# Reordering the front of a two-layer cross-attention kernel: load queues, K by halves, output operand on GpSimd, roots by pair, and the first score slots

## The reference

```python
q, k, v = tgt @ Wq.T, memory @ Wk.T, memory @ Wv.T        # per head, 16 heads
x = x + attention(q, k, v)[0]                             # sequence 0 alone, added to all 32
norm_X   = layernorm(ctx) * norm1_w + norm1_b
norm_F_L = layernorm(x)   * norm2_w + norm2_b
attended = softmax(norm_F_L @ norm_X.T * scale) @ norm_X
cross    = gelu(attended @ fc1_w.T + fc1_b) @ fc2_w.T + fc2_b
norm_c   = layernorm(cross) * norm3_w + norm3_b
out      = norm_F_L + gamma2 * (cross + gamma1 * softmax(norm_c @ norm_c.T * scale) @ norm_c)
```

## Time and profile before

| | |
|---|---|
| median of 3 runs | 245.54 us (245.11 to 245.64) |
| the profiled execution | 245.04 us, its span 243.1 us |
| PE busy in the span | 219.4 us (90%) |
| DVE busy | 187.5 us (77%) |
| ACT busy | 151.6 us (62%) |
| POOL busy | 140.6 us (58%) |
| DMA moved | 26.81 MB |

### The profile page before, as it was taken

How to read it: one execution, slowest core, us unless ns; L and a number is a source line. 1 busy time by engine, 2 the same in 40 slices (tenths; PEclk the granted TensorE clock), 3 DMA queues, 4 the chain that set the end, 5 groups by cost and what they waited for, 6 DMA issues and landing times.

```text
span 243.1 us, 5101 instructions
## 1 busy us (share of the span) xinstructions
PE 219.4 (90%) x1812; PEld 161.4 (66%) x1812; DVE 187.5 (77%) x363; ACT 151.6 (62%) x292; POOL 140.6 (58%) x212
## 2 busy tenths in 40 slices
PE   6989989697999999999999899999989988979860
PEld 6856647475878789787896777967667654454420
DVE  6888858899999987798799999933423767857773
ACT  2166866216778768776787976855684646657520
POOL 6000086676999999969878957500079885201340
PEclk9999999989999999999999999999999999999985
DMA  5990000154553525544145000000000024333468
GB/s 164 377 368 3 1 1 3 44 173 131 173 174 100 161 90 173 175 133 164 52 172 173 3 0 4 0 1 3 0 3 1 0 96 156 141 131 140 171 230 326
DMA packets 14712, 26.81 MB, mean 110 GB/s; under 512 B 1760, under 2 KB 1760, under 8 KB 14688
## 3 DMA queue, kind: packets, MB, share of 16 engines
q1 hardware_dynamic: 14688, 26.50, 32.0%
HBM read 18.11 MB, written 8.39 MB: 109 GB/s over the span
## 4 chain that ended last, share of the span: by engine, by line
PE 61%; DVE 20%; POOL 6%; issue 6%; ACT 5%; DVEq 0%; ACTq 0%; POOLq 0%
PE psum L1042 16%; PE psum L979 8%; PE psum L934 6%; PE psum L1050 5%; DVE bn L372 5%; DVE xN L392 5%; PE psum L1080 3%; PE psum L1160 2%; PE psum L1062 2%; PE psum L992 2%; DVE Fall L586 2%; DVE nmax L531 2%; PE psum L1007 2%; PE psum L1020 2%; PE psum L949 2%
## 5 line engine op out<-in xcount | busy, mean ns | idle before, releaser
L1042 PE MATMUL psum<-XT,Fall 128*128 128x256 f32 x256 | 62.5, 388 | 1.8 <-ACT Fall L822 1.8
L1042 PEld LDWEIGHTS psum<-XT,Fall 128*128 128x128 f32 x256 | 47.2, 195 | 7.6 <-ACT Fall L822 2.2
L665 POOL TENSOR_SCALAR cN<-cN,nmean,rstd 128x256 f32<-128x256 f32 x64 | 38.9, 618 | 2.4 <-POOL rstd L652 2.3
L645 POOL TENSOR_TENSOR xN<-xN,tgt 128x512 f32<-128x512 f32 x28 | 35.7, 1277 | 1.6 <-DVE xN L392 1.6
L845 ACT ACTIVATE PT<-psum 128x512 f32<-128x512 f32 x32 | 19.2, 599 | 24.4 <-PE psum L1050 24.2
L392 DVE TENSOR_SCALAR xN<-xN,bn,rstd 128x256 f32<-128x256 f32 x64 | 33.7, 571 | 0.7 <-POOL rstd L652 0.7
L652 POOL TENSOR_TENSOR rstd<-vps,minus_half 128x8 f32<-128x8 f32 (+1 forms) x16 | 25.0, 1564 | 15.2 <-DVE vps L383 15.1
L852 ACT ACTIVATE E<-psum,nmax 128x256 f32<-128x256 f32 x64 | 26.8, 476 | 10.7 <-DVE nmax L531 10.6
L531 DVE TENSOR_REDUCE nmax<-psum 128x2 f32<-128x512 f32 x32 | 22.0, 686 | 13.9 <-PE psum L1042 13.3
L934 PE MATMUL psum<-ident 128*128 128x128 f32 x198 | 29.9, 297 | 2.8 <-POOL ident L617 1.9
L934 PEld LDWEIGHTS psum<-ident 128*128 128x128 f32 x198 | 25.4, 201 | 7.2 <-issue 5.2
(11 more groups left out here) (174 smaller groups left out, 357.0 us busy)
## 6 DMA issues: line engine op xcount, KB each, us to landing
cN<-ctx SPq DMA_DIRECT2D x32, 256.0 KB, 3.0
xN<-x SPq DMA_DIRECT2D x32, 256.0 KB, 4.0
out<-Fall SPq DMA_DIRECT2D x32, 256.0 KB, 2.3
x0T<-x0t SPq DMA_DIRECT2D x1, 256.0 KB, 2.7
wqT<-wqt SPq DMA_DIRECT2D x1, 256.0 KB, 3.1
c0T<-c0t SPq DMA_DIRECT2D x1, 256.0 KB, 4.0
wkT<-wkt SPq DMA_DIRECT2D x1, 256.0 KB, 4.9
wvT<-wvt SPq DMA_DIRECT2D x1, 256.0 KB, 5.0
```

The costliest lines, as they stand in the source:

```text
L645: pool.tensor_tensor(xN[:, b % SLOTS, :], xN[:, b % SLOTS, :], tgt2[:, :, :].rearrange("p t d -> p (t d)"), ALU.add).then_inc(y_ok, 1)
L665: pool.tensor_scalar(own, own, nmean[:, p % 4, NT * m + t:NT * m + t + 1], root_of(p, 0, m, t), ALU.add, ALU.mult)\
L1042: last = pe.matmul(bank[SBANK1[b % 3]][:, t * N:(t + 1) * N], Fall[:, b, c, t * P:(t + 1) * P], XT[:, p % 4, c, m * N:(m + 1) * N], start= ...
```

## The change

It has these parts:

- **Loads.** ACT issues `x0T` and `c0T`; SP issues the parameters, the three weights, then all eight context sequences, then all eight x sequences.
- **Start of PE.** The dummy products use `meanw`, which is now GpSimd's first memset, and are eight instead of seven.
- **K by halves.** K's two halves go to two banks with a semaphore step each; DVE masks the first half before the first scores and the second half in slot 0. V's first half is projected behind the first scores and its second half in slot 2; ACT copies them in slots 1 and 3.
- **Operand products.** They move from the front of PE to the place behind the turned context pairs, with `project(0)`, seven dummy products and `project_back(0)` around them (there were 11 dummy products there). DVE copies their result ahead of its first `normal`.
- **Output operand.** It leaves DVE (7 small instructions ahead of the K mask, 4 behind it, 4 in slot 18) and becomes 17 small instructions on GpSimd behind its memsets.
- **Roots by pair.** The first six context sequences get variances, root and normalisation pair by pair within the attention slots.
- **Score slots.** DVE takes `maximum(b)` first in every slot. Statistics and x-side normals of the first slots come later and are caught up in slots 4 and 5. POOL's `add(5)` waits for the fourth DVE normal.

The diff, cut to its core:

```diff
@@ sync
-        for dst, src, arrived in ((x0T, x0t, q_in), (wqT, wqt, q_in), (c0T, c0t, k_in), (wkT, wkt, k_in),
-                                  (wvT, wvt, v_in)):
-            sp.dma_start(dst[:, :, :], src).then_inc(arrived, 16)
+        sp.dma_start(wqT[:, :, :], wqt).then_inc(q_in, 16)
+        sp.dma_start(wkT[:, :, :], wkt).then_inc(k_in, 16)
+        sp.dma_start(wvT[:, :, :], wvt).then_inc(v_in, 16)
+
+        for src, dst, arrived in ((c_d, cN, c_in), (x_d, xN, x_in)):
+            for b in range(SLOTS):
+                sp.dma_start(dst[:, b, :], src[b, :, :]).then_inc(arrived[b], 16)
@@ vector
-        output_operand(0)
-        dve.wait_ge(k_mm, 1)
-        for e, m in enumerate(("even", "odd")):
-            dve.tensor_scalar(kTm[:, e, :, :], tiles(bank[1]), c_(m), None, ALU.mult).then_inc(kT_ok, 1)
+        def masked(o):
+            dve.wait_ge(k_mm, o + 1)
+            for e, m in enumerate(("even", "odd")):
+                dve.tensor_scalar(kTm[:, e, o, :], bank[(1, 5)[o]][:, 0:N], c_(m), None, ALU.mult).then_inc(kT_ok, 1)
...
         add(2)
         add(3)
+        dve.wait_ge(qk_mm, 1)
+        link(dve.tensor_copy(Q[:, :], bank[7][:, 0:(H + 1) ** 2]))
+        link(dve.tensor_copy(K[:, :], bank[7][:, 64:64 + U * U]), "QK")
         normal(0)
         normal(1)
...
-        statistics(5, 1)
-        variances(2)
...
         for b in range(B):
             k, m, q = b // 2, b % 2, b // 4
-            if k + 3 < PAIRS:
-                statistics(b + 6, 0)
-                statistics(b + 6, 1)
-                if m == 1:
-                    variances(k + 3)
             maximum(b)
...
-            if k + 2 < PAIRS:
+            if b == 0:
+                statistics(2 * EARLY - 1, 1)
+                variances(EARLY - 1)
+            if b in (2, 3, 4):
+                normal(b + 3)
+            if 1 <= b <= 4:
+                statistics(b + 5, 0)
+                statistics(b + 5, 1)
+                if m == 0:
+                    variances((b + 5) // 2)
+            if b >= 4 and b + 6 < B:
+                statistics(b + 6, 0)
+                statistics(b + 6, 1)
+                if m == 1:
+                    variances((b + 6) // 2)
+            if b == 1:
+                normal(4)
+            elif b == 5:
+                normal(8)
+                normal(9)
+            elif 6 <= b < B - 4:
                 normal(b + 4)
@@ gpsimd
+        pool.memset(meanw[:, :], 1.0 / D).then_inc(consts, 1)
...
+            if b == 5:
+                pool.wait_ge(zy_ok, 8)
...
-        for b in range(2 * EARLY):
-            normal(b)
+        for p in range(EARLY):
+            pool.wait_ge(vps_first, 2 * p + 2)
+            pool.tensor_tensor(rstd[:, p, 0, :], vps[:, p, 0, :], minus_half[:, 0:2 * NT], ALU.pow).then_inc(root_first, 1)
+            normal(2 * p)
+            normal(2 * p + 1)
@@ scalar
+        act.dma_start(x0T[:, :, :], x0t).then_inc(q_in, 16)
+        act.dma_start(c0T[:, :, :], c0t).then_inc(k_in, 16)
@@ tensor
-        keep_busy(11, 7)
...
+        project(0)
+        operand_products()
+        keep_busy(3, 0)
+        project_back(0)
+        keep_busy(4, 0)
         turned(0, 1)
```

More of the change, by code:

```diff
@@ L52 @@
 QUADS = B // 4
+EARLY = 3
 SLOT = 64
@@ L338, in _ @@
                                        src[:, c, :].unsqueeze(1).to_broadcast([P, n, n]), ALU.mult), "prods")
[L340 to L352, removed]
-        output_operand(0)
-        dve.wait_ge(k_mm, 1)
-        for e, m in enumerate(("even", "odd")):
-            dve.tensor_scalar(kTm[:, e, :, :], tiles(bank[1]), c_(m), None, ALU.mult).then_inc(kT_ok, 1)
[L358 to L361, removed]
+        def masked(o):
+            dve.wait_ge(k_mm, o + 1)
+            for e, m in enumerate(("even", "odd")):
+                dve.tensor_scalar(kTm[:, e, o, :], bank[(1, 5)[o]][:, 0:N], c_(m), None, ALU.mult).then_inc(kT_ok, 1)
+        masked(0)
         stats = [0]
@@ L408, in _ @@
             if p < NHP:
+                if p == 0:
+                    masked(1)
                 if p < 2 * EARLY:
                     statistics(p, 0)
[L411 to L418, removed]
+                if p in (1, 3, 5):
+                    first_variances(p // 2)
         dve.wait_ge(o0_mm, NHP // 2)
@@ L638, in _, with step @@
         pool.memset(sC[:, :, SC:SLOT], 0.0).then_inc(zero_ok, 1)
+        oc = [0]
+        def step(ins):
+            ins.then_inc(operand_ok, 1)
+            oc[0] += 1
+            pool.wait_ge(operand_ok, oc[0])
+        a5 = c_("a5").rearrange("p (c k) -> p c k", c=DC)
+        pool.wait_ge(zero_ok, 4)
+        pool.wait_ge(alg, ALG["prods"])
+        step(pool.tensor_tensor(g12[:, :], c_("g1"), c_("g2"), ALU.mult))
+        for c in range(DC):
+            step(pool.tensor_scalar(Rt[:, c, 0:H], a5[:, c, 0:H], c_("g2", c), None, ALU.mult))
+            step(pool.tensor_scalar(Rt[:, c, H:CO], MT[:, c, :], g12[:, c:c + 1], None, ALU.mult))
+            step(pool.tensor_scalar(Rcut[:, c, 0:1], a5[:, c, H:H + 1], c_("g2", c), None, ALU.mult))
+            step(pool.tensor_tensor(Rt[:, c, CO - 1:CO], Rt[:, c, CO - 1:CO], Rcut[:, c, 0:1], ALU.add))
+        for part in range(2):
+            to = stR[:, :, part, :]
+            step(pool.tensor_copy(slots(to, CO, SLOTS_L[0]), repeated(Rt[:, :, :], 3)))
+            step(pool.tensor_tensor(Rcut[:, :, :], Rt[:, :, :], to[:, :, 0:CO], ALU.subtract))
+            step(pool.tensor_copy(slots(to, CO, SLOTS_L[1]), repeated(Rcut[:, :, :], 2)))
+            step(pool.tensor_tensor(to[:, :, 5 * CO:6 * CO], Rcut[:, :, :], to[:, :, 3 * CO:4 * CO], ALU.subtract))
+        ALG["stR"] = oc[0]
         def add(b):
@@ L862, in _ @@
             evacuate(p, 0)
+        turned_values(0)
         evacuate(0, 1)
@@ L870, in _ @@
             exponentials(b)
-            if b % 4 == 1:
+            if b % 4 == 1 and q >= 1:
                 turned_values(q)
```

86 lines of the change are left out of this document (48 added, 38 removed).

## The result

The changed kernel takes 251.39 us in the median of 4 runs (250.08 to 251.98), against 245.59 (245.11 to 247.34) for the kernel before in the same series. The ratio is 1.0225, with a 95% interval of 1.0182 to 1.0269: slower, by 5.8 us. The forecast was 250.6 us, and its range of 243.5 to 252.8 holds the time. The profiled execution took 251.32 us with a span of 249.4; before, the span was 243.1.

What follows compares the result with a forecast made beforehand. DVE was taken to bound the x-side preparation, PE the score slots. On 245.04 us: -0.6 (X3 earlier), +3.8 (chain to X4), +3.5 (clock), -1.05 (late slots) = +5.6, so 250.6 us; range 243.5 to 252.8.

Steps and rivals of the forecast that it cites:

- Front, 1.9 us of t0: From the span's start to DVE's first x-side normal: that normal was forecast about 1.9 us earlier than 44.12.
- t0: Start of DVE's first x-side normal, at 44.12 us in the kernel before; forecast about 1.9 us earlier.
- t0 to X3, 20.2 us: First x-side normal to the turn of context pair 3: forecast 20.2 us, 1.3 more than before.
- X3: Start of PE's turn of context pair 3, at 63.00 us before; forecast about 0.6 us earlier.
- X3 to X4, 11.3 us by the chain: Turn of context pair 3 to that of pair 4: everything in a row, 11.3 us against 7.49, 3.8 lost.
- X4: Start of PE's turn of context pair 4, at 70.49 us before; forecast 11.3 us behind X3.
- Two clock falls, 3.5 us: Scores behind X3 and X4: PE's longer waits lower its clock, costing 2 x 1.76 = 3.5 us; bounds 0 and 5.5.
- Late slots, -1.05 us: Slots 20 to 29: maximum ahead of statistics frees PE of waits of 0.80 and 0.25 us, 1.05 gained.
- one fall: Rival on the chain from X3 to X4: only one clock fall on the path, 249.0 us; one or none, chance 0.25.
- The first score also falls: Rival: first score at the lower clock, first two maxima and X3 1 us later, 251.6 us; included in 0.52.
- late loads: Rival in the front: loads land late, 1 us less gain, 251.6 us; included in the 0.52.
- The chain is covered: Rival: PE sets X4 again if X3 is before about 59.3, front's gain stays, 242.1 us; chance 0.18.

Runs made afterwards that it cites:

- waits filled: Changed kernel with seven dummy products on PE in each of the two waits ahead of and within the turn of context pair 3: 250.88 us, ratio 1.0227.
- old front with the new slots: Kernel before, with only the new order of statistics, variances and normals in DVE's score slots: 254.25 us, ratio 1.0374.
- five edits: The three edits, with four and two dummy products, plus sequence 6's statistics in slot 0 and GpSimd's normal 7 ahead of add(9), on the changed kernel: 244.33 us.
- old order from slot 6: Changed kernel with statistics and variances ahead of the maximum again from slot 6 on: 249.15 us, ratio 1.0149.
- one queue: Changed kernel with x0T and c0T issued by SP again, so all loads in one queue: 254.12 us in one run.
- nine edits: The five edits plus sequence 8's statistics earlier, normal 7 in slot 3, GpSimd's normal 9 ahead of add(11), dummy products around side x, pair 2: 242.95 us.
- three edits: Changed kernel with sequence 9's statistics and pair 4's variances in slot 3, dummy products in pair 3's waits, old order from slot 6: 245.36 us.

## Why the prediction came out right

The direction, the place and nearly the size: +5.8 us measured, +5.6 summed. By its steps:

- *Front, 1.9 us of t0:* measured 1.63. The first scores came 0.3 later than counted, since Q's products took 2.57 us, where I had counted on some of the time at a higher clock. The granted clock reads 1.00 all through the front, so no row shows such a change there. The adds (1.29) and the copies' short wait (0.24) were as counted.
- *t0 to X3, 20.2 us:* measured 20.10. The four points that were named on the way came as told: normals 2 and 3 in 1.38, the first maximum at 47.94 (48), DVE's wait for `add(5)`, the root of pair 3 at 57.19 (t0 + 14.70).
- *X3 to X4, 11.3 us by the chain:* 13.17 with the clock, and 10.98 if the turn and the score behind X3 are put at their full-clock times (1.33 to 0.87, 3.66 to 1.93). The waits of DVE and POOL show the ring, and moving two statistics and two small instructions cuts it. The kernel with the waits filled measured 10.82 for the same chain.
- *Two clock falls, 3.5 us:* **mis-sized.** One fall, on the path, of 2.2 us (1.73 in the score and 0.46 in the turn; 2.35 by the kernel with the waits filled). I had taken the waits ahead of X3 and X4 to be alike and each to bring a fall. In the profile after only the first did; in that of the old front with the new slots only the second did.
- *Late slots, -1.05 us:* **wrong in sign**, +1.0 measured. The step failed where it took PE's waits for ACT's copies as the end of a chain through DVE's maximum. The longer one lies in a stretch in which ACT works without a wait, two table loads among it, and it stayed. What the new order did was to put the variances behind the maximum, which made POOL's roots and normals later, and PE waited for these too.

With one fall of 2.2 and late slots of +1.0 the sum would have been -0.4 + 3.5 + 2.2 + 1.0 = 6.3, the difference of the spans. The two errors (1.3 too much, 2.1 too little) happened to cancel for the most part: that the number came so close is luck in these two terms, while the chain from X3 to X4 came as it was worked out.

The rival that came nearest was "one fall", at 249.0; with the late term as measured it would have read about 251. "The first score also falls" did not come (2.00 us at 45.90), nor did late loads. "The chain is covered" failed at its own condition: X3 was 62.59, not before 59.3 (59.2, by its own terms). The sentence of the Trainium skill that stood with it ("Perfetto Trace Analysis", section "Identifying Performance Opportunities") is not borne out here by the busy share alone: DVE was the busiest (9.93 of 10 us) and was relieved of 1.9 us. Of that 0.9 showed between t0 and X3, by the kernel without the wait of `add(5)`, and the time went up all the same, since a new chain of waits took more.

Open: why the same waits bring a fall of the clock in one execution and not in another. The waits of 1.10 and 0.84 ahead of the score of slot 3 were followed by one in two profiles (five edits: 55.43, and the old order from slot 6) and not in five others. Of the six profiles with the waits of 0.41 and 1.80 ahead of X4, three had a fall at X3 and none at X4 (after, old order from slot 6, no wait of add(5)), three the reverse (old front, waits filled, one queue). Late in the span the clock fell at 224 us with one queue and at 231 with the waits filled, behind waits of PE of 0.30 to 0.55 us that the changed kernel has too, without a fall.

## What to carry to other kernels

When an instruction is moved behind a wait on an in-order engine, write down what the awaited engine itself waits for: here DVE's variances moved behind a maximum, the maximum needs PE, PE needs GpSimd, and GpSimd needs the variances, so four links that had run side by side came one after the other. Put what only feeds a later stage (statistics, roots) into the idle time ahead of such a wait, and the short thing that the next engine stands waiting for first; one order for all slots was not the best in either kernel. And an edit that brings one stage forward is worth only what the next bound leaves of it: the same front brought X3 forward by 2.9 us with one order of the slots and by 0.7 with the other.

## What the runs showed of the hardware that was not expected

A fall of TensorE's clock does not keep its place: with dummy products in the waits at X3 the granted clock stayed at 1.00 there, and fell behind X4 instead (score 3.31 us), where in the changed kernel, behind the same 1.80 us of waiting, it had stayed up (1.89). In all four profiles with dummy products at X3 the score behind it took 1.89; with the same waits of 1.67 and 1.80 unfilled it took 3.5 to 3.6 us in three profiles and 1.89 in two, so that filling kept the clock up is likely and not shown. In the profiles of this case, only when no wait of more than 0.55 us was left from the turn of side x, pair 2 to X4 (nine edits), or the waits at X3 were filled and X4 had none (three edits), was there no fall in the slots at all.
